# Moving the last stage's first two batches into the last two items of the attention stage

## What is computed

```python
    # second attention, per batch b and group g of 4 heads (8 groups)
    scores = jnp.einsum('bqhd,bkhd->bhqk', q, k_all) * SCALE
    scores = jnp.where(valid[:, None, None, :], scores, -1e+30)
    probs = jax.nn.softmax(scores, axis=-1)
    o = jnp.einsum('bhqk,bkhd->bqhd', probs, v_all)
    o = o.reshape(bsz, seqlen, HQ * D)
    return jnp.einsum('bse,de->bsd', o, Wo)
    ...
    # last stage
    out = jnp.einsum('bsd,od->bso', hidden_states, W) + b
    scores = x @ gate_w.T + gate_b
    probs = jax.nn.softmax(scores, axis=-1)
    routing_weights, selected = jax.lax.top_k(probs, TOPK)
    lora_outputs = jnp.stack([x @ A[:r, :].T @ B[:, :r].T for r in RANKS], axis=1)
```

## Time and profile before

| | us |
|---|---|
| median of 3 runs | 1378.03 (1377.44 to 1378.14) |
| profiled execution, its own time | 1379.38 |
| span of its profile | 1377.6 |
| TensorE busy | 1320.8 |
| VectorE busy | 1073.6 |
| ScalarE busy | 862.2 |
| GpSimd busy | 652.7 |

### The profile page before, as it was taken

One profiled execution on the slowest core, in us unless ns is written; L12 is line 12 of the kernel. 1 busy time (PEld: TensorE's weight loads), 2 busy tenths in 40 slices (PEclk: granted clock), 3 DMA queues, 4 the chain that ended last, 5 costly groups with the idle time before them and its releaser, 6 DMA issues.

```text
span 1377.6 us, 26519 instructions
## 1 busy us (share of the span) xinstructions
PE 1320.8 (96%) x8104; PEld 1135.1 (82%) x8104; DVE 1073.6 (78%) x2962; ACT 862.2 (63%) x2500; POOL 652.7 (47%) x649
## 2 busy tenths in 40 slices
PE   5789997899999999999999999999999999999988
PEld 4656675588888888888888888888888888888878
DVE  3767767588888888888788888888878888888766
ACT  1567776566666666667666766676666666666631
POOL 1345546454635364536444654365345545553521
PEclk9889999999999999999999999999999999999999
DMA  8434444454121212121212122312212121212121
GB/s 279 149 116 152 154 162 131 146 130 139 32 62 32 77 32 62 32 77 32 62 32 78 36 58 45 80 39 54 61 48 62 32 77 32 62 31 66 34 77 62
DMA packets 196400, 107.59 MB, mean 78 GB/s; under 512 B 140961, under 2 KB 180898, under 8 KB 195106
## 3 DMA queue, kind: packets, MB, share of 16 engines
q1 hardware_dynamic: 195248, 105.71, 28.5%
q10 hardware_dynamic: 1010, 0.17, 0.1%
HBM read 101.66 MB, written 37.75 MB: 101 GB/s over the span
## 4 chain that ended last, share of the span: by engine, by line
PE 89%; DVE 5%; ACT 2%; issue 2%; POOL 1%; DMA 0%; SPq 0%; DVEq 0%; ACTq 0%; POOLq 0%
PE ps L1209 12%; PE ps L1211 12%; PE ps L1210 12%; PE ps L1260 10%; PE ps L1281 5%; PE ps L1274 5%; PE ps L1275 5%; PE ps L1294 4%; PE ps L1293 4%; PE ps L1300 4%; PE ps L258 2%; PE ps L1236 2%; PE ps L246 2%; ACT a_pr L432 1%; PE ps L305 1%
## 5 line engine op out<-in xcount | busy, mean ns | idle before, releaser
L1406 ACT ACTIVATE b_pf<-b_sm,b_nb,b_rstd 128x640 f32<-128x640 f32 x256 | 235.1, 918 | 102.0 <-DVE b_nb L1511 101.8
L1412 ACT ACTIVATE b_p_h<-ps 128x640 fp32r<-128x640 f32 x256 | 180.5, 705 | 181.9 <-PE ps L1260 181.2
L1525 DVE TENSOR_TENSOR b_p_l<-ps,b_p_h 128x640 fp32r<-128x640 f32 x256 | 210.7, 823 | 81.2 <-ACT b_p_h L1412 74.0
L1504 DVE CUSTOM_DVE_ANT_0 b_sm<-ps,mask_row 128x640 f32<-128x640 f32 x256 | 209.3, 817 | 1.3 <-issue 0.4
L1260 PE MATMUL ps<-ident,b_pf 128*128 128x128 f32 x1280 | 181.7, 273 | 7.8 <-DVE b_p_l L1525 4.8
L1209 PE MATMUL ps<-b_w_h,x1t_h 128*128 128x512 f32 (+1 forms) x512 | 179.5, 350 | 2.3 <-issue 2.0
L1520 DVE TENSOR_SCALAR b_pf<-b_pf,b_ri 128x640 f32<-128x640 f32 x256 | 158.3, 618 | 28.4 <-DVE b_ri L1517 1.4
L1209 PE MATMUL ps<-b_kt_h,b_qt_h 128*128 128x320 f32 x512 | 174.1, 340 | 1.2 <-DVE b_mx L1504 1.2
L1260 PEld LDWEIGHTS ps<-ident,b_pf 128*128 128x128 f32 x1280 | 152.1, 140 | 27.2 <-issue 6.0
L1210 PE MATMUL ps<-b_w_l,x1t_h 128*128 128x512 f32 (+1 forms) x512 | 173.5, 339 | 0.0
L1211 PE MATMUL ps<-b_w_h,x1t_l 128*128 128x512 f32 (+1 forms) x512 | 172.9, 338 | 0.0
(11 more groups left out here) (167 smaller groups left out, 3234.1 us busy)
## 6 DMA issues: line engine op xcount, KB each, us to landing
kv_of_batch<-in_kv SPq DMA_DIRECT2D x128, 256.0 KB
b_ck<-kv_of_batch SPq DMA_DIRECT2D x64, 256.0 KB, 3.7
b_cv<-kv_of_batch SPq DMA_DIRECT2D x256, 64.0 KB, 2.2
raw<-in_w SPq DMA_DIRECT2D x32, 384.0 KB, 5.4
raw<-in_wo SPq DMA_DIRECT2D x32, 256.0 KB, 3.6
a_xt<-in_xt SPq DMA_DIRECT2D x8, 256.0 KB, 5.5
a_xin<-in_x SPq DMA_DIRECT2D x8, 256.0 KB, 5.6
x<-a_x SPq DMA_DIRECT2D x8, 256.0 KB, 5.1
```

The lines of the kernel that those rows point to most:

```text
L1406: act.activation(pf[:, h % 2], sm[:, h % 2], ACT.Exp, bias=nb[:, m.b % 2, h:h + 1], scale=rstd[:, m.b % 4, h:h + 1], accum_out=rs[:, m.b % ...
L1412: act.activation(p_h[:, :, h * P:(h + 1) * P], turned_row, ACT.Copy).then_inc(ph_sb, 1)
L1504: dve.tensor_tensor_reduce(sm[:, h % 2], score_row, mask_row[:, m.b], 1.0, MASKED, ALU.add, ALU.max, mx[:, k, h:h + 1]).then_inc(mx_sb, 1)
L1525: dve.tensor_tensor(p_l[:, :, cols], turned_row, p_h[:, :, cols], ALU.subtract).then_inc(pl_sb, 1)
```

## The change

The functions of stage 3 are handed out one by one instead of in bundles, and steps of batches 0 to 2 are placed elsewhere on three engines:

- TensorE: `turn(0)` in slot 62 between the probabilities of (62, 0) and (62, 1); `turn(1)` at the end of slot 62, ahead of the probabilities of (62, 3); `gate(0)` in slot 63 between the probabilities of (63, 0) and (63, 1); `rest(0)` at the end of slot 63, ahead of the probabilities of (63, 3). Behind these come `turn(2)` and `gate(1)`, then the values of item 63, `low_rank(0)` and the output product.
- ScalarE: `h_out(0)` in slot 62 ahead of the copy of (62, 2), `h_out(1)` in slot 63 ahead of the first exponent, `h_out(2)` ahead of `split_b`.
- VectorE: `h_rest(0)` in slot 62 ahead of the subtraction of (62, 2), `h_rest(1)` in slot 63 ahead of the reciprocal of (63, 1), `h_rest(2)` behind `choose(0)` and ahead of `output(end)`.
- Banks: `gate(0)` writes bank 7 instead of 1, and the first low-rank transpose bank 3 instead of 7. The waits that guard them move along: `turn(0)` waits for `qtl_sb` of all items, `gate(0)` for `knl_sb`, `rest(0)` and `gate(1)` for `mx_sb`, `rest(1)` and `low_rank(0)` for `pl_sb`.

What the code calls the same step stands on other lines afterwards: L1260 becomes L1252, L923 L925, L929 L931, L1293 L1285, L1417 L1418, L997 L989, L1016 L1008.

```diff
@@ -850,18 +850,18 @@
 
 
 def phase3(nc, ctx, t, ident, w_h, w_l, x1t_l, cw, sw, raw, hacc, x1_dram, out, ps, x1_out,
-           k_ps, qab_sb, kab_sb, wql_sb, wkvl_sb, mx_sb, pl_sb, ol_sb, h_sb):
+           k_ps, qab_sb, kab_sb, wql_sb, wkvl_sb, qtl_sb, knl_sb, mx_sb, pl_sb, ol_sb, h_sb):
 
     sb = lambda n, s, d=F32: ctx.enter_context(nc.sbuf_tensor("c_" + n, s, d))
     sem = lambda n: ctx.enter_context(nc.semaphore("c_" + n))
     NX = NR + MAXR
     DONE = G * B
     CUT = W3 // 2
-    F, GL = (0, 2, 4), (1, 3, 5)
+    F, GL = (0, 2, 4), (7, 1, 5, 3, 1, 5, 3, 1)
     first_of = lambda b: ps[:, F[b % 3], 0:CUT]
-    second_of = lambda b: ps[:, GL[b % 3], 0:CUT]
-    gate_of = lambda b: ps[:, GL[b % 3], D - CUT:CUT]
-    lowt_of = lambda b: ps[:, LT, 0:P]
+    second_of = lambda b: ps[:, GL[b], 0:CUT]
+    gate_of = lambda b: ps[:, GL[b], D - CUT:CUT]
+    lowt_of = lambda b: ps[:, LT if b else 3, 0:P]
     rows_of = lambda b: ps[:, F[b % 3], :]
     HT, LT = 6, 7
 
@@ -918,6 +918,8 @@
 
     def turn(pe, b):
         wait(pe, htl_sb, b)
+        if b == 0:
+            pe.wait_ge(qtl_sb, DONE)
         pe.wait_ge(h_sb, DONE - B + b + 1)
         for i in range(KT):
             mm = pe.transpose(ps[:, HT, i * P:(i + 1) * P], hacc[:, b, i * P:(i + 1) * P], ident[:])
@@ -936,9 +938,9 @@
         if b == 0:
             pe.wait_ge(wql_sb, KT * (G + 1))
             pe.wait_ge(wkvl_sb, G + 1)
+            pe.wait_ge(knl_sb, DONE)
+        if b == 1:
             pe.wait_ge(mx_sb, REP * DONE)
-        if b == 1:
-            pe.wait_ge(pl_sb, REP * DONE)
         if b == 2:
             pe.wait_ge(ol_sb, DONE)
             pe.wait_ge(h_sb, DONE)
@@ -946,10 +948,16 @@
         product(pe, b, second_of(b), slice(CUT, W3), True).then_inc(gl_ps, 1)
 
     def rest(pe, b):
+        if b == 0:
+            pe.wait_ge(mx_sb, REP * DONE)
+        if b == 1:
+            pe.wait_ge(pl_sb, REP * DONE)
         product(pe, b, first_of(b), slice(0, CUT), False).then_inc(f_ps, 1)
 
     def low_rank(pe, b):
         pe.wait_ge(low_sb, b + 1)
+        if b == 0:
+            pe.wait_ge(pl_sb, REP * DONE)
         pe.transpose(lowt_of(b), flat(low[:, b % 2]), ident[:]).then_inc(lowt_ps, 1)
 
     def add_low_rank(pe, b):
@@ -960,22 +968,6 @@
             pe.matmul(rows_of(b)[:, cols], lowt[:, b % 2], bt_h[:, cols], start=False, stop=False)
             mm = pe.matmul(rows_of(b)[:, cols], lowt[:, b % 2], bt_l[:, cols], start=False, stop=cols.stop == D)
         mm.then_inc(done_ps, 1)
-
-    def begin(pe):
-
-        turn(pe, 0)
-
-    def first_rows(pe):
-
-        gate(pe, 0)
-        rest(pe, 0)
-        turn(pe, 1)
-
-    def more_rows(pe):
-
-        turn(pe, 2)
-        gate(pe, 1)
-        low_rank(pe, 0)
 
     def batches(pe):
         rest(pe, 1)
@@ -1007,7 +999,7 @@
 
     def rows_act(act):
         for b in range(B):
-            if b + 2 < B:
+            if 0 < b < B - 2:
                 h_out(act, b + 2)
             low_out(act, b)
 
@@ -1068,7 +1060,7 @@
             pool.wait_ge(ht_ps, b + 1)
             pool.tensor_tensor(hacc[:, b], x1[b], b_ffn, ALU.add).then_inc(xb_sb, 1)
 
-    return ((load_small, load, store), (begin, first_rows, more_rows, batches), (h_out, split_b, rows_act),
+    return ((load_small, load, store), (turn, gate, rest, low_rank, batches), (h_out, split_b, rows_act),
             (h_rest, choose, rows_dve), prepare)
 
 
@@ -1147,7 +1139,7 @@
         end = Item(G - 1, B - 1)
         sp_ffn, pe_ffn, act_ffn, dve_ffn, pool_ffn = phase3(
             nc, ctx, t, ident, w_h, w_l, x1t_l, cw, sw, raw, hacc, x1_dram, out, ps, x1_out,
-            k_ps, qab_sb, kab_sb, wql_sb, wkvl_sb, mx_sb, pl_sb, ol_sb, h_sb)
+            k_ps, qab_sb, kab_sb, wql_sb, wkvl_sb, qtl_sb, knl_sb, mx_sb, pl_sb, ol_sb, h_sb)
         block = ctx.enter_context(nc.Block())
 
         @block.sync
@@ -1300,6 +1292,8 @@
                     mm = pe.matmul(ps[:, SM, :], o_l[:, h * P:(h + 1) * P], wo_h[:, h], start=False, stop=h == REP - 1)
                 mm.then_inc(wo_ps, 1)
 
+            turn_rows, gate_rows, rest_rows, low_rows, batches = pe_ffn
+
             def slot(m, one, two, last):
                 if last:
                     turn_probs(last, 3)
@@ -1315,6 +1309,10 @@
                     turn_probs(m, 0)
                 if two:
                     project_q(two)
+                if m.n == end.n:
+                    gate_rows(pe, 0)
+                if m.n == end.n - 1:
+                    turn_rows(pe, 0)
                 if m:
                     turn_probs(m, 1)
                 if one:
@@ -1331,16 +1329,19 @@
                     out_of_lows(last)
                 if two:
                     project_kv(two)
+                if m.n == end.n - 1:
+                    turn_rows(pe, 1)
+                if m.n == end.n:
+                    rest_rows(pe, 0)
 
             tensor_first(pe, (project_q, project_kv, turn_q, turn_new, scores))
-            begin, first_rows, more_rows, batches = pe_ffn
             slots(pe, slot)
-            begin(pe)
             turn_probs(end, 3)
-            first_rows(pe)
+            turn_rows(pe, 2)
+            gate_rows(pe, 1)
             values_of_highs(end)
             values_of_lows(end)
-            more_rows(pe)
+            low_rows(pe, 0)
             out_of_highs(end)
             out_of_lows(end)
             batches(pe)
@@ -1416,11 +1417,15 @@
                 wait(act, wo_ps, m.n)
                 act.activation(o_h[:], ps[:, OT, :], ACT.Copy).then_inc(oh_sb, 1)
 
+            h_out, split_b, rows_act = act_ffn
+
             def slot(m, one, two, last):
                 if one:
                     new_kv(one)
                 if last:
                     high(last, 3)
+                if m.n == end.n:
+                    h_out(act, 1)
                 if one:
                     queries(one)
                 if m and m.b == 6:
@@ -1447,6 +1452,8 @@
                     high(m, 1)
                 if one:
                     new_keys(one)
+                if m.n == end.n - 1:
+                    h_out(act, 0)
                 if two:
                     squares(two)
                 if m:
@@ -1457,11 +1464,9 @@
                         q_weights(m.g + 1, c)
 
             scalar_first(act, (q_weights, kv_weights, squares, new_kv, queries, cache_keys, new_keys, cache_values))
-            h_out, split_b, rows_act = act_ffn
             slots(act, slot)
-            h_out(act, 0)
             high(end, 3)
-            h_out(act, 1)
+            h_out(act, 2)
             split_b(act)
             output(end)
             rows_act(act)
@@ -1534,6 +1539,8 @@
                     dve.tensor_copy(hacc[:, m.b], ps[:, SM, :]).then_inc(h_sb, 1)
                     return
                 dve.tensor_tensor(hacc[:, m.b], ps[:, SM, :], hacc[:, m.b], ALU.add).then_inc(h_sb, 1)
+
+            h_rest, choose, rows_dve = dve_ffn
 
             def slot(m, one, two, last):
                 if last:
@@ -1546,6 +1553,8 @@
                 if m:
                     invert(m, 0)
                     bias(m, 1)
+                if m.n == end.n:
+                    h_rest(dve, 1)
                 if one:
                     queries(one)
                 if m:
@@ -1566,6 +1575,8 @@
                     bias(m, 3)
                 if two:
                     rope_products(two)
+                if m.n == end.n - 1:
+                    h_rest(dve, 0)
                 if m:
                     low(m, 2)
                     invert(m, 3)
@@ -1586,14 +1597,11 @@
                 dve.tensor_tensor(w_l[:, :, cols], raw[:, :, cols], w_h[:, :, cols], ALU.subtract).then_inc(wkvl_sb, 1)
 
             vector_first(dve, (rope_products, new_values, queries, new_keys, maxima, low_weights, low_kv_weights))
-            h_rest, choose, rows_dve = dve_ffn
             slots(dve, slot)
-            h_rest(dve, 0)
             low(end, 3)
-            h_rest(dve, 1)
             choose(dve, 0)
+            h_rest(dve, 2)
             output(end)
-            h_rest(dve, 2)
             accumulate(end)
             rows_dve(dve)
 
```

## The result

| | before | after |
|---|---|---|
| median, us | 1378.24 (1377.44 to 1379.41, 6 runs) | 1373.38 (1372.1 to 1374.0, 6 runs) |
| profiled execution, us | 1379.38 | 1372.97 |
| span of its profile, us | 1377.6 | 1371.2 |

The ratio of after to before is 0.9965, with a 95% interval of 0.9955 to 0.9975: the change takes 4.86 us off, 0.35%. The forecast was 1374.4 us. It was worked out from the first three runs of before, with a median of 1378.03 us; three more moved that median to 1378.24 us.

What follows compares the result with a forecast made beforehand. TensorE was taken as the bound, busy for 96% of the span, with pauses left to fill from 1305 to 1347 us. 0.35 + 3.33 + 0.73 - 0.80 = 3.61 us off the 1378.03 us median gave 1374.4 us, range 1372.6 to 1376.2.

Steps and rivals of the forecast that it cites:

- Where the time is lost: TensorE's pauses from 1305 to 1347 us, the last two items and first batches: busy for 35.82 of 42 us.
- Steps 1 to 4: turn(0), turn(1), gate(0), rest(0) fit into TensorE's pauses in items 62 and 63: gains nothing, 0.35 us, and 3.33 us together.
- Step 6: TensorE waits for ScalarE's copy L1417 before the output product, with only low_rank(0) left to cover it: cost 0.80 us.
- The sum: TensorE's gains less the new wait, 0.35 + 3.33 + 0.73 - 0.80: the end comes 3.61 us earlier.
- step 5: gate(0)'s wait on TensorE for the VectorE subtraction of L1016, behind the probabilities of (63, 3), goes: gain 0.73 us.
- The covers: Idle time on ScalarE and VectorE hides the four moved copies and subtractions: cost nothing, 2.52 us if uncovered.
- (c): Item 63's two thin covers fail, turn(1)'s copy and subtraction delay the softmax chain: 1.26 us back, 1375.7 us; chance 0.10.
- (e): gate(0) waits for its subtraction ahead of the probabilities of (63, 1), so nothing overlaps: slower, 1381.4 us; chance 0.03.
- The clock: Behind the 2.07 us pause before (62, 1) the granted clock falls to 0.50, costing 1.55 us; turn(0) shortens the pause.
- rival (a): The clock fall was in the median of before too and goes: 1372.9 us; chance 0.14.
- both roads: Profiled execution less 3.61 and the fall's 1.55 us gives 1374.2 us; median, taken without fall, less 3.61 gives 1374.4 us.
- The rule on transposes: Transposes do not count as busy TensorE, so turn(0) could not stop the clock fall: profiled 1375.8 instead of 1374.2 us.

Runs made afterwards that it cites:

- e8: The changed kernel with three plain matmuls of 512 columns more behind gate(0), in the trip (63, 0) to (63, 1); 1374.1 us.
- e5: The changed kernel with gate(0) taken out of the trip (63, 0) to (63, 1) and put ahead of rest(0); 1374.58 us.
- e6: The changed kernel with rest(0) behind the probabilities of (63, 3) instead of ahead; 1374.31 us.
- e3: The changed kernel with turn(0) behind the probabilities of (62, 1) and the key transpose instead of ahead of them; 1375.08 us.
- e2: The kernel before with two plain matmuls of 512 columns added in the pause ahead of the probabilities of (62, 1); 1377.12 us.
- e1: The kernel before with four transposes added in the pause ahead of the probabilities of (62, 1); 1377.55 us.

## Why the prediction held, and where it was off

- **Where the time is lost**: right. The tail did not change, and the head varies from one execution to the next whatever the kernel; what the change gives came out of the stretch.
- **Steps 1 to 4**: right. The trips stayed at 2.45 and 3.26 us. The room of 0.27 us named for gate(0) showed in e8: 0.70 us more cost 0.39 us, where the sum gave 0.43. e5 and e6 gave back 1.39 and 1.61 us, where the sum gave 1.55 and 1.6; most of the 0.16 us short in e5 is in the price of 3.33 us for gate(0) and rest(0), which held a slow start behind a pause.
- **Step 6, the new wait**: right in place and size. From 1334.89 + 0.03 to 1335.74 it is 0.82 us, for 0.80 forecast. Splitting gate(1) took 0.77 to 0.81 us off.
- **The sum**: 3.61 us forecast, 3.53 us measured. The term that was mis-sized is step 5: turn(2) starts 0.61 us behind the start of the probabilities of (63, 3), and not the 0.47 us assumed, so 0.59 us went there and not 0.73. The value products gave 0.08 us of it back: 3.49 us from 1331.40 to 1334.89, against 3.57 us before.
- **The covers**: right. The ScalarE and VectorE steps behind the moved ones have 0.47 and 0.48 us of idle time left; rivals (c) and (e) fall.
- **The clock**: the size was right, 1.58 us for 1.55, and so was the guess that turn(0) would take the fall away. What failed is the choice of the median: "I take it that the median mostly lacks the fall". All three profiles of before have it, and seven of the 11 runs of e3 lie in the group that looks like it. The 1.35 us between the profiled execution and the median were no fall but a long head: 1305.47 us, the longest of all 14 profiles. The other two, with the same fall and heads of 1304.68 and 1305.09 us, came to 1378.60 and 1379.02 us, shorter by just what their heads are shorter. So rival (a), given a chance of 0.14, described what happens. The forecast of 1374.4 us was 1.0 us too high for want of the fall; rival (a)'s 1372.9 us was 0.5 us too low, of which 0.2 us is the median of before, which moved up with more runs, and 0.1 us the sum.
- **That both roads met** at 1374.2 and 1374.4 us was chance, and the number came out in the range although this choice was wrong. The road of the profiled execution had the fall right but carried that execution's long head: after's profiled execution took 1372.97 us with a head 1.32 us shorter. The road of the median had a usual head and no fall.
- **Do some runs of before lack the fall?** An estimate: without one, e2's stretch of 40.17 us with the shortest head, 1303.11 us, the tail and the 1.8 us outside the span would make 1375.5 us. With a fall it would be 1377.0 us, and with the longest head 1379.4 us; a run with no fall and the longest head would be at 1377.9 us. The 60 timed runs of before lie between 1376.91 and 1379.64 us, 42 of them above 1377.85 us, so most had a fall, at one place or the other, and for the rest the times can't tell. The measured 4.86 us need no such runs to lie 0.22 us below the 5.08 us of the stretch: heads scatter by 2.4 us, and each median is of six runs.
- **The rule on transposes** (the Trainium skill, TensorE: Matmul & The Clock Gate, Part 4: PE-mode transpose) was said to leave the fall in place. The trace does not agree: in after TensorE ran only transposes from 1304.15 to the scores at 1307.57 us, as long as before, and four more transposes in that time were enough in nine profiles of nine. By the medians of e1 and e2 a filler of plain matmuls was 0.4 us better; e1's profile has the fall at the second place and e2's has none. Each is a single execution, and their heads differ by 1.3 us (1303.54 and 1304.84 us), so whether the filler or the execution made that difference was not tested.

## What to carry to other kernels

A round trip between engines through one buffer has a fixed length: add up the work that stands in it, and independent work is free up to the difference, to within 0.2 us here, and costs its full length beyond. When a filler is moved from where it covered something, look for the wait it leaves behind, and split it if two waits need it. Of a pause on TensorE count also the clock behind it; and before you put a difference of 1 us between a profile and a median down to one cause, profile the same kernel two or three times and cut the span into parts.

## What the runs showed of the hardware

A small VectorE operation took four to almost six times as long beside a GpSimd one, and ended with it. `choose` has an operation on 4 columns (L1027, L1019 in after) that takes 223 ns in the median of its eight calls. VectorE and GpSimd of after, in order of time:

```profile
1331.39 1.24 DVE L1019 SCALAR_TENSOR_TENSOR c_weight<-c_sc,c_top,c_first 128x4 f32<-128x4 f32 x1
```

```profile
1331.33 1.29 POOL L1057 TENSOR_TENSOR x1t_l<-raw,x1t_l 128x512 fp32r<-128x512 f32 x1 [21.37 <-ACT x1t_l L998]
```

It took 1.24 us and ended at 1332.63, when GpSimd's subtraction ended at 1332.62. In before the same pair stood at 1338.39 for 0.88 us and ended 0.02 us behind GpSimd's. The Trainium skill (GPSIMD Engine Reference, Specifications) says that GpSimd shares its SBUF interfaces with VectorE and contends with VectorE instructions that have two SBUF inputs. This operation has two (`c_sc` and `c_first`), and the trace agrees. It cost nothing here: the transpose of `low_rank`, which needs what follows from it, starts at 1334.89 us, 2.3 us later, and had no idle time ahead of it.
